# Gathers paced by landings, token rows turned two experts ahead into two banks, hidden values turned after the scatter

## The reference, cut to what matters

```python
logits = x @ router_weight.T                      # 512 tokens x 64 experts
topw, topi = top_k(softmax(logits), 8)            # topw normalised to sum 1
xe[e, slot] = x[token]                            # 64 experts x 128 slots x 256
gu = xe @ gate_up_proj[e]                         # 256 -> 192, all fp32
h = silu(gu[:96]) * gu[96:]
ye = h @ down_proj[e]                             # 96 -> 256
y[token] = sum over its 8 experts of topw * ye[expert, slot]
out = x + tanh(g_ffn) * y
```

## Time and profile before

| what | us |
|---|---|
| median of 3 runs | 226.35 |
| the three runs | 223.43, 226.35, 227.15 |
| the profiled execution's own time | 225.09 |
| its span, first to last instruction | 223.3 |
| PE busy in the span | 209.1 (94%) |
| ACT busy | 110.4 (49%) |

### The profile page before, as it was taken

One profiled execution on the slowest core, in us unless ns is written; L12 is line 12 of the kernel. 1 busy time (PEld: TensorE's weight loads), 2 busy tenths in 40 slices (PEclk: granted clock), 3 DMA queues, 4 the chain that ended last, 5 costly groups with the idle time before them and its releaser, 6 DMA issues.

```text
span 223.3 us, 5260 instructions
## 1 busy us (share of the span) xinstructions
PE 209.1 (94%) x1676; PEld 166.2 (74%) x1676; DVE 140.0 (63%) x443; ACT 110.4 (49%) x350; POOL 105.5 (47%) x145
## 2 busy tenths in 40 slices
PE   7889999999999779899999899998989999999983
PEld 3556767776557247688998798888879888999973
DVE  6366354476498976637666665656666656348765
ACT  2525445434634926555555564645665555444431
POOL 7301222222262457555655556575555754756630
PEclk9999999999999999999999999999999999999999
DMA  5699999999011234787898898988755655223222
GB/s 153 191 301 282 305 283 250 246 251 236 23 59 23 68 103 128 208 222 217 237 288 245 255 250 276 246 252 276 212 141 160 173 157 157 73 70 83 84 70 94
DMA packets 37725, 41.03 MB, mean 184 GB/s; under 512 B 3874, under 2 KB 35044, under 8 KB 37700
## 3 DMA queue, kind: packets, MB, share of 16 engines
q1 hardware_dynamic: 32932, 27.21, 43.8%
q0 software_dynamic: 4048, 12.98, 22.0%
q10 hardware_dynamic: 720, 0.52, 0.8%
HBM read 32.97 MB, written 7.74 MB: 182 GB/s over the span
## 4 chain that ended last, share of the span: by engine, by line
PE 69%; DVE 8%; DMA 8%; issue 6%; ACT 3%; POOL 2%; another core or an unknown queue 2%; ACTq 0%; DVEq 0%; POOLq 0%
PE bank L789 13%; PE scores L807 10%; PE bank L779 8%; PE scores L779 6%; PE scores L769 6%; PE bank L574 5%; PE bank L589 4%; PE bank L813 4%; DMA gate_w<-xn_dram,slot_token 3%; PE scores L555 3%; DMA gate_w<-in_ctx_dram 3%; PE bank L518 2%; PE bank L537 2%; DMA xe<-xn_dram,slot_token 2%
## 5 line engine op out<-in xcount | busy, mean ns | idle before, releaser
L497 POOL DMA_INDIRECT gate_w<-xn_dram,slot_token x56 | 57.7, 1031 | 40.4 <-issue 15.0
L789 PE MATMUL bank<-y_high,scatter 128*128 128x256 f32 x156 | 45.0, 315 | 0.1
L789 PE MATMUL bank<-y_low,scatter 128*128 128x256 f32 x156 | 39.7, 281 | 0.0
L1280 DVE TENSOR_SCALAR scatter<-tokens,slot_token 128x256 fp32r<-128x256 f32 (+1 forms) x64 | 24.9, 390 | 22.9 <-PE bank L789 19.2
L807 PE MATMUL scores<-down_all,work 96*128 96x256 f32 x128 | 38.2, 380 | 0.7 <-DVE y_low L1293 0.7
L1003 ACT ACTIVATE gate_w<-scores,gate_w 128x256 f32<-128x256 f32 x42 | 20.0, 475 | 27.9 <-PE scores L807 16.3
L428 POOL TENSOR_SCALAR_AFFINE_SELECT gate_w<-gate_w 128x256 f32<-128x256 f32 x32 | 12.2, 406 | 44.2 <-ACT gate_w L904 44.2
L789 PEld LDWEIGHTS bank<-y_high,scatter 128*128 128x128 f32 x156 | 29.5, 189 | 2.3 <-issue 0.5
L789 PEld LDWEIGHTS bank<-y_low,scatter 128*128 128x128 f32 x156 | 29.8, 191 | 0.1
L779 PE MATMUL scores<-gate_w,work 128*128 128x192 f32 x128 | 26.5, 329 | 0.9 <-ACT work L978 0.9
L779 PE MATMUL bank<-gate_w,work 128*128 128x192 f32 x128 | 26.5, 330 | 0.4 <-ACT work L978 0.4
(11 more groups left out here) (193 smaller groups left out, 338.1 us busy)
## 6 DMA issues: line engine op xcount, KB each, us to landing
gate_w<-_L_ffn_gate_up_proj_dram SPq DMA_DIRECT2D x8, 768.0 KB, 10.8
down_all<-in_L_ffn_down_proj_dram SPq DMA_DIRECT2D x16, 384.0 KB, 9.2
gate_w<-_L_ffn_gate_up_proj_dram SPq DMA_DIRECT2D x32, 192.0 KB
ye_dram<-gate_w SPq DMA_DIRECT2D x42, 128.0 KB
gate_w<-xn_dram,slot_token POOLq DMA_INDIRECT x56
ye_dram<-xe SPq DMA_DIRECT2D x5, 128.0 KB
x_sb<-in_x_dram SPq DMA_DIRECT2D x2, 256.0 KB, 4.7
ye_dram<-xn SPq DMA_DIRECT2D x3, 128.0 KB
```

The costliest lines, as they stand in the source:

```text
L497: pool.indirect_dma_start(out=rows, out_offset=None, in_=xn2_dram, in_offset=bass.IndirectOffsetOnAxis(ap=slot_token[:, e:e + 1], axis=0), ...
L789: last = nc.tensor.matmul(bank[6 + t // 2][:, t % 2 * H:t % 2 * H + H], scatter[e % 2][:, t * P:t * P + P], (y_high, y_low)[part][e % 2][: ...
L1280: v.tensor_scalar(scatter[e % 2][:, 0:wide], tokens[:, 0:wide], slot_token[:, e:e + 1], None, ALU.is_equal).then_inc(scatter_done, 1)
```

## The change

It does four things.

1. Gathers (POOL): `pace_tokens`, the wait for the copy of `e-3` and the wait for expert `e-8` go. In their place gather `e` waits until gather `e-2` has landed, or `e-3` for experts 10 to 39, so that at most two or three are on their way.
2. Turning rows ahead (PE and ACT): from step 11 on the rows of expert `s+2` are turned and copied in step `s`, behind the gate-up product and the Silu (step 11 does two, experts 12 and 13). Up to step 10 the order is as before.
3. Two banks: rows of odd experts from 13 to 49 are turned into bank 7, all others into bank 1. A turning waits for the copy of the last expert that used the same bank.
4. `turn_hidden` of `s-1` stands after the scatter instead of ahead of it, in steps 11 to 63.

```diff
+AHEAD_FROM = 12
-PACED_FROM = 10
...
+        def on_the_way(e):
+            return 3 if SINGLES + 3 <= e < RESERVED + XE_SEMS else 2
...
+        def rows_turned_in(e):
+            return 7 if AHEAD_FROM < e < EARLY and e % 2 else 1
+        def turned_ahead(s):
+            if s < ROWS_LAST:
+                return (s + 1,)
+            if s < AHEAD_FROM - 1:
+                return ()
+            return tuple(e for e in ((s + 1, s + 2) if s == AHEAD_FROM - 1 else (s + 2,)) if e < E)
...
-                if e >= XE_SEMS:
-                    pool.wait_ge(xe_in[e % XE_SEMS], 16 * (e // XE_SEMS))
                 if free_after:
                     pool.wait_ge(gu_mm, free_after)
-                if 3 <= e < PACED_FROM:
-                    pool.wait_ge(xeT_done, e - 2)
-                elif e >= PACED_FROM:
-                    pace_tokens(e - PACED_FROM)
+                landed = e - on_the_way(e)
+                if landed >= 0:
+                    pool.wait_ge(xe_in[landed % XE_SEMS], 16 * (landed // XE_SEMS) + 16)
...
                 pe.wait_ge(xe_in[e % XE_SEMS], 16 * (e // XE_SEMS) + 16)
-                if e:
-                    pe.wait_ge(xeT_done, e)
+                same_bank = [d for d in range(e) if rows_turned_in(d) == rows_turned_in(e)]
+                if same_bank:
+                    pe.wait_ge(xeT_done, same_bank[-1] + 1)
...
-                if s + 1 < E and not 0 <= s < ROWS_LAST:
+                if s < 0 or ROWS_LAST <= s < AHEAD_FROM - 1:
                     turn_rows(s + 1)
                 if 0 <= s < E:
                     gate_up_of(s)
-                if 0 <= s < ROWS_LAST:
-                    turn_rows(s + 1)
-                if 0 <= s - 1 < E:
+                    for e in turned_ahead(s):
+                        turn_rows(e)
+                if 0 <= s - 1 < E and (s < AHEAD_FROM - 1 or s >= E):
                     turn_hidden(s - 1)
...
                         scatter_of(e)
+                if AHEAD_FROM - 1 <= s < E:
+                    turn_hidden(s - 1)
                 if 0 <= s - 2 < E:
                     down_of(s - 2)
```

More of the change, by code:

```diff
@@ L454, in _ @@
             pool.wait_ge(xn2_stored, 16 * (QT + len(ROUTES)))
[L455 to L471, removed]
             def pace_rows(c):
@@ L764, in turn_rows @@
                 pe.wait_ge(xe_in[e % XE_SEMS], 16 * (e // XE_SEMS) + 16)
-                if e:
-                    pe.wait_ge(xeT_done, e)
+                same_bank = [d for d in range(e) if rows_turned_in(d) == rows_turned_in(e)]
+                if same_bank:
+                    pe.wait_ge(xeT_done, same_bank[-1] + 1)
                 rows = xe_of(e)[0][:, 0:H].rearrange("s (c p) -> s c p", c=KC)
                 for c in range(KC):
-                    last = nc.tensor.transpose(bank[1][:, c * P:c * P + P], rows[:, c, :], ident[:])
+                    last = nc.tensor.transpose(bank[rows_turned_in(e)][:, c * P:c * P + P], rows[:, c, :], ident[:])
                 last.then_inc(xe_turned, 1)
@@ L977, in keep_rows @@
                     act.wait_ge(gu_mm, e - 1)
-                copy(xeT[e % 2].rearrange("p k t -> p (k t)"), bank[1][:, 0:KC * P]).then_inc(xeT_done, 1)
+                copy(xeT[e % 2].rearrange("p k t -> p (k t)"), bank[rows_turned_in(e)][:, 0:KC * P]).then_inc(xeT_done, 1)
             def gate(e):
@@ L990, in _ @@
                     gate(s)
-                if 0 <= s < ROWS_LAST:
-                    keep_rows(s + 1)
+                    for e in turned_ahead(s):
+                        keep_rows(e)
                 if 0 <= s - 1 < E:
```

## The result

The changed kernel takes 235.05 us (median of 4 runs, 233.67 to 236.3) against 226.74 of the kernel before beside it: ratio 1.0458, 95% interval 1.0351 to 1.0565. Every ratio here leaves out executions more than 1.5% over the fastest of the same kernel (in this one 227.13 and 227.15 us of the kernel before), so it is not the quotient of the medians, which is 1.037 here. The forecast was 221.1 (218.0 to 226.5). The prediction was wrong: the time lies outside its range, on the side that had 0.13.

A forecast was written before the change was run, and what follows sets the result against it. PE was taken as the bound: 5.35 us of its waits, less 1.05 leaking through, plus 0.2 from the gathers, gave 4.5 us won; from the runs' mean of 225.64 that made 221.1 us, range 218.0 to 226.5.

The forecast's parts named there:

- the side that had 0.13: The outcome that the change makes the whole kernel measurably slower, given a chance of 0.13.
- The floor, and where PE waits: PE's work per step, experts 12 to 63: at least 1.89 us, or 2.37 with eight scatter matmuls; waits sit in few steps.
- That is all the change can win there: Gate-up 12 to 63: 106.32 us against a floor of 100.97, so 5.35 us of PE waits bound the gain.
- Part 1, the order: Turning rows ahead into two banks removes PE's waits for the copy just before, except 1.05 us leaking in three late steps.
- half is given back: Rival: ACT's late instruction still costs PE at scatter or hidden transpose; 2 to 3 us won, 222.5 to 224; chance 0.23.
- I take neither: Fewer gathers might shorten ACT's lateness (1.05 us more won) or steady ones make it oftener; neither was counted.
- Part 2: Hidden transpose behind the scatter on PE: cost zero, with 1.4 us of cover; without it up to 0.25 us a step.
- Part 3, the head: Early gathers: gather 8 goes between 0.3 us earlier and 0.25 later; gather 11 goes 1.7 earlier, PE seeing 0.1 to 0.2.
- Part 3, the lead: With three gathers on their way, one goes every 1.24 to 1.54 us, so the lead grows about 0.2 gathers a step.
- 8 experts in hand, 15 us: Lead of the gathers over PE at expert 40, of which 6 us would be used by the end.
- Part 3, who waits: On POOL only gathers and row gathers stand behind a waiting gather, and PE's turning waits for these; 0.2 us won overall.
- The slower one: Rival: a steady stream of gathers keeps ACT late in every step, adding 9.6 us, about 230 us; chance 0.16.

The follow-up runs named there:

- sets 2 to 4: Three of four groups of follow-up runs, each on one chip with the kernel before beside it, whose medians there are 219.71, 219.11 and 219.17 us.
- e1: The changed kernel with the old waits of the gathers, keeping the new order on PE and ACT: 224.26 us, ratio 1.0021.
- e2: The kernel before, old order kept, with only its gathers' waits as in the changed kernel: 236.99 us, ratio 1.0663.
- e3: The changed kernel with three gathers on their way for experts 40 to 63 as well: 230.5 us, ratio 1.0334.
- set 3: Group of follow-up runs with the changed kernel and the kernel before both profiled on one chip; median of the kernel before 219.11 us.
- a1: The changed kernel without an edit, run and profiled again beside the kernel before on one chip: 232.36 us, ratio 1.0583.
- e14: The changed kernel with DVE's row adds three steps later each: 231.52 us, ratio 1.0562.
- e9: The changed kernel with the old waits for the first ten gathers and three on their way from gather 10 to the last: 219.18 us, ratio 1.0018.
- b1: The kernel before without an edit, run again for its profile: 219.52 us, ratio 1.0012.
- e4: The changed kernel with the old waits for gathers 0 to 9, the landing rule starting at expert 10: 233.32 us, ratio 1.0485.
- e6: The changed kernel with all of DVE's row adds behind the last expert: 231.84 us, ratio 1.0546.

## Why the prediction was wrong, step by step

**The floor, and where PE waits: right.** 1.89 and 2.37 us are the floor of a step with the change too; most of the steps from 12 to 46 of the changed kernel have it.

**"That is all the change can win there": right as a bound, wrong as a property of the kernel.** The 5.35 us came from one profiled execution on one chip. On the three chips of sets 2 to 4 no such waits appear (101.30 to 101.36 us from 12 to 63 in the kernels with the old order and an early end, against the floor of 100.97).

**Part 1, the order: right that it does no harm, wrong on what it wins.** Of the 5.35 us, 4.3 were put down to turning ahead. In e1 the stretch from 12 to 63 still takes 105.16 us against 106.32, a gain of about 1.2 across chips, and none in the median. In its profiled execution the long steps are others (14, 25, 38, 44 and 51, up to 2.87 us), and what PE waits for in them stands ahead of the hidden transpose, as the rival "half is given back" had it; its gain of 2 to 3 us did not come. In the middle the limit on the gathers did the work, as far as e1 and e2 tell. The step that failed is "I take neither" on whether fewer gathers shorten ACT's lateness. The rule weighed there (the Trainium skill, "SBUF — State Buffer", "Who interferes with whom") speaks of accesses to SBUF. ACT's late instruction lasts its ordinary 0.47 us and is late in starting; what these rows show late is a start, so the rule gave no ground for "neither". No run here shows the ports.

**Part 2: right for the changed kernel.** No gap of it outside the end is put down to the moved transpose. Where ACT is late, the cover can be short: PE waits ahead of it for 1.9 us in four places in e1, and for 1.8 in four in e3.

**Part 3, the head: wrong.** Gather 8 was reckoned from 6 and 7 at their old places, "between 0.3 won and 0.25 lost". But 2 already waits for 0 to land, and each later one for the one two before. It slipped 3.4 us, gather 9 behind it 3.7, and the stretch up to gate-up 8 grew by 3.7 (2.9 in set 3).

**Part 3, the lead: wrong.** "With three on their way that gives a gather every 1.24 to 1.54 us" divided a latency by three. In a1 gather 11 goes at 98.54 and gather 40 at 151.79: 1.84 us each, hardly under a step's 1.89. Two things were missing. The landing took longer than was reckoned: for the gathers from 98 to 152 us 3.7 to 5.5 us, median 4.3. And a gather does not go at the landing that it waits for, but 0.77 us behind it. (4.3 + 0.77)/3 is 1.7, most of the way to 1.84. The list of POOL's waits in a1 seems to name another limit, a gate-up product that has to free a buffer, 21.9 us in 19 waits:

```profile
POOL gate_w L492 <- DMA gate_w<-xn_dram,slot_token: 21.7, 19, 1.8
POOL gate_w L492 <- PE scores L775: 13.6, 10, 2.0
POOL gate_w L492 <- PE bank L775: 8.3, 9, 2.0
```

It is a wait for several semaphores put down to the wrong one. Every gather from 10 on finds its buffer free at least 7 us before it goes: gather 38, for one, goes at 147.29 in step 32 and needs only the gate-up products of the first 26 experts. For two gathers of every eight (2, 3, 10, 11, 18, 19 and so on) this trace has no landing. In 14 of the 19 cases the landing that was waited for is there, and the gather goes 0.77 or 0.78 us behind it. So the buffers are no limit here; the landings are.

So the lead hardly grew. Gather 40 was issued 6.4 us ahead of its turning (158.17), some 3 of them left after landing, and not "8 experts in hand, 15 us". The next term held better: 23 gathers from 151.79 to 200.99 took 2.14 us each, where "2.3" was said.

**Part 3, who waits: the step that decided.** "Behind the waiting gather on POOL stand only later gathers and, after them, the row gathers; who waits for these is PE's turning." PE's turning does not wait for the row gathers. DVE's row adds do, in the middle of steps 59 to 63, with `hide` behind them, and at the very end the result does. The prediction's own numbers would have shown it: the last token gather at about 143 + 55 = 198 (40 issued eight steps of 1.89 ahead of its turn, near 158), sixteen row gathers at 1.31 to 219, 3.7 to land: 223, about the whole span of the kernel before, and some 4.5 us of adds and output follow the last landing (e14: 225.7 to 230.3), so a span near 227. So even with the lead that was hoped for, the 4.5 us could not have come; with the lead that there was (151.79 + 23 x 2.14 = 201) the rows land at 226. The tail was called "the same" without this sum; in set 3 the late queue cost 6.7 us from 59 to 63 and 2.7 behind them.

**The rivals.** The slower one had the right sign and nearly the size (230), by a mechanism that did not occur, so the nearness is luck: in the changed kernel the list of ACT's waits from 106 to 196 us has no unnamed releaser ahead of L1001 any more, and two short ones elsewhere (1.7 and 0.5 us). A late queue on POOL was no rival at all, which is why its chance was too small.

## What to carry to other kernels

When a queue gets a limit on what is on its way, carry its issue times on to the last item of the queue, and ask of every kind of item behind the limited ones who waits for it and what stands behind that waiter. A limit of n on their way does not give latency/n each: the time from the landing to the issue comes on top (2.14 us each with two and a median of 3.4 us to land, 1.84 with three and 4.3). When the profile names a releaser for a wait on several semaphores, check in the code whether that one had long been satisfied. And when taking a wait away leaves the time as it was, look for a second limit beside it before calling the wait harmless.

## What the runs showed of the hardware that was not expected

A gather goes 0.77 us after the landing that it waits for, as the changed kernel's chain shows (174.88 + 3.45 = 178.33, and the next at 179.10), so with two on their way a pair costs 3.36 + 0.77 us, 2.07 us each:

```profile
174.88 3.45 DMA gate_w<-xn_dram,slot_token
...
178.40 0.71 issue
179.10 3.36 DMA gate_w<-xn_dram,slot_token
```

The landings took longer with more gathers on their way: for the last 24 token gathers the median is 3.4 us in a1 (two on their way) and 3.8 in e9 (three), on the same chip, one execution each.

The kernel before loses 5 us in the middle, PE behind late starts of ACT, in the first profile, and 0.3 to 0.4 on three other chips. The kernel before in the first profile, ACT's waits from 106 to 196 us (line, what it waited for: us in all, times, longest):

```profile
ACT gate_w L1003 <- remote: 4.2, 3, 1.8
```

In b1 the same question is answered with no "remote" at all. In the first profile of the changed kernel and in e4, ACT heard of gate-up 61 3.6 us after it was free for it; in a1, e6 and e14, with the same unbroken run of row gathers, it did not. Each set ran on one chip, so chip and time of day can't be told apart, and what holds these signals up stays open.
